# Third layer of a four-layer network: the attention's denominators kept with heads on partitions and spread on strips of the array, and the last batch's squares summed ahead of the down projection

## The reference

```python
def _L2_attn_ref(x, w_qkv, w_out, decay_param):      # 16 heads of 16 channels
    q = _phi(to_bhtd(q))                             # phi(z) = elu(z) + 1
    k = _phi(to_bhtd(k))
    running_kv = _decay_scan(k * v, decay, init)     # s_t = decay * s_{t-1} + x_t
    running_ksum = _decay_scan(k, decay, init)
    den = jnp.clip(jnp.sum(q * running_ksum, axis=-1, keepdims=True), EPS_DEN, None)
    out = q * running_kv / den
    out = out.transpose(0, 2, 1, 3).reshape(B, T, Hid) @ w_out

def _L2_ffn_ref(x, w_gate_up, w_proj):
    h = jax.nn.silu(gate) * up                       # 1024 wide, ternary weights
    hn = rms_norm(h)
    return jnp.einsum('bsd,hd->bsh', hn, wq_p)
```

## Time and profile before

| quantity | us |
|---|---|
| median of 3 runs | 1033.42 |
| lowest and highest of them | 1028.28, 1034.17 |
| the profiled execution's own time | 1029.84 |
| its span, first to last instruction | 1028.0 |
| TensorE busy in the span | 946.4 |
| VectorE busy | 715.1 |
| ScalarE busy | 464.8 |
| GpSimd busy | 435.2 |

### The profile page before, as it was taken

One profiled execution on the slowest core, in us unless ns is written; L12 is line 12 of the kernel. 1 busy time (PEld: TensorE's weight loads), 2 busy tenths in 40 slices (PEclk: granted clock), 3 DMA queues, 4 the chain that ended last, 5 costly groups with the idle time before them and its releaser, 6 DMA issues. The chain is left out here.

```text
span 1028.0 us, 12619 instructions
## 1 busy us (share of the span) xinstructions
PE 946.4 (92%) x4494; PEld 481.0 (47%) x4498; DVE 715.1 (70%) x1327; ACT 464.8 (45%) x767; POOL 435.2 (42%) x444
## 2 busy tenths in 40 slices
PE   4999799879999999878999997999999999999997
PEld 2677555323333333344555646633662474256325
DVE  3777565678888888547777773768586777758674
ACT  2333045247766666645575451621371246134411
POOL 2222357554444333017245361087128505840770
PEclk9999799979999999998999997999999999999999
DMA  8700035312211220030000001000000000000000
GB/s 295 259 16 16 16 105 141 123 40 65 63 47 49 63 63 2 1 146 1 17 16 1 16 1 44 1 0 1 21 1 1 1 21 1 0 1 22 0 1 21
DMA packets 28942, 43.67 MB, mean 42 GB/s; under 512 B 6512, under 2 KB 22080, under 8 KB 28480
## 3 DMA queue, kind: packets, MB, share of 16 engines
q1 hardware_dynamic: 28880, 42.87, 13.4%
HBM read 31.38 MB, written 11.27 MB: 41 GB/s over the span
## 5 line engine op out<-in xcount | busy, mean ns | idle before, releaser
L2180 POOL TENSOR_TENSOR l_scaled<-l_X,l_source 128x512 f32<-128x512 f32 x112 | 135.6, 1240 | 141.6 <-ACT l_X L2250 124.6
L1102 DVE TENSOR_REDUCE l_nmax<-banks 128x1 f32<-128x512 f32 (+1 forms) x165 | 147.7, 929 | 34.9 <-PE banks L1211 33.7
L1057 ACT ACTIVATE l1b_PT<-banks 128x512 f32<-128x512 f32 (+1 forms) x176 | 134.1, 793 | 66.8 <-PE banks L1224 66.4
L1211 PE MATMUL banks<-l_KQ 96*128 96x512 bf16 x240 | 81.3, 392 | 8.6 <-DVE l_nmax L1102 5.8
L1224 PE MATMUL banks<-l_KQ 99*128 99x512 bf16 x256 | 85.0, 385 | 3.0 <-ACT l1b_PT L1057 2.1
L2263 ACT ACTIVATE l_hhi<-l_h 128x512 f16<-128x512 f32 (+1 forms) x24 | 15.1, 630 | 129.4 <-DVE l_h L2375 129.4
L2599 PE MATMUL banks<-l_scaled,l_cbm 128*64 128x512 f32 x224 | 59.5, 613 | 10.7 <-POOL l_scaled L2180 10.6
L1238 PE MATMUL banks<-l1b_PT,l1b_V 128*32 128x512 f32 x512 | 68.2, 605 | 0.0
L2349 DVE TENSOR_TENSOR l_decayed<-banks,l_right_decay 128x512 f32<-128x512 f32 x56 | 38.4, 686 | 37.9 <-PE banks L2599 37.9
L2621 PE MATMUL banks<-l_decayed,w_place 64*128 64x512 f32 x224 | 63.2, 641 | 0.0
L1783 PE MATMUL banks<-l_xhi,l_ternary 128*128 128x512 f16 x128 | 49.8, 389 | 8.6 <-DVE l_h L1713 8.6
(11 more groups left out here) (342 smaller groups left out, 2052.1 us busy)
## 6 DMA issues: line engine op xcount, KB each, us to landing
l_split<-l1a_parts SPq DMA_DIRECT2D x16, 384.0 KB, 3.3
l_KQ<-l_split SPq DMA_DIRECT2D x48, 128.0 KB, 2.9
l_KQ<-l_split SPq DMA_DIRECT2D x16, 192.0 KB, 3.1
l_KQ<-l_split SPq DMA_DIRECT2D x48, 64.0 KB, 2.8
w_ternary<-l_tern_out SPq DMA_DIRECT2D x7, 384.0 KB, 2.3
x<-in_x SPq DMA_DIRECT2D x4, 512.0 KB, 9.4
l_raw<-in_w_gate_up SPq DMA_DIRECT2D x2, 1024.0 KB, 9.9
out<-x SPq DMA_DIRECT2D x4, 512.0 KB, 3.0
```

The costliest lines, as they stand in the source:

```text
L1057: nc.scalar.activation(PT[:, first:first + size, :], source, ACT.Exp, scale=SCALE).then_inc(p_ready, 1)
L1102: nc.vector.tensor_reduce(nmax[:, H % 2, first:first + size], source, axis=AX.X, op=ALU.max, negate=True).then_inc(smax_read, 1)
L1211: last = nc.tensor.matmul(ps[bank + m][:, :], KQ[pairs, QUERY, g, j, t * P:(t + 1) * P], KQ[pairs, KEY, g, j, :], start=True, stop=True)
L2180: nc.gpsimd.tensor_tensor(by_head(scaled[:, (2 * u + m) % 4, :]), by_head(X[:, T, :]), spread(source[:, level, T, :]), ALU.mult).then_inc( ...
```

## The change

The selector gets 32 columns instead of 8 (the further 24 are zeros), and the denominators are made with heads on partitions at once: two products (four instructions) of 512 columns, one on columns 0 to 31 of the array and one on columns 32 to 63, which fill partitions 0 to 63 of bank 6. The column of the ternary mean moves to bank 7. VectorE clips 64 partitions of 512 columns in one instruction and waits for it (semaphore `den_read`). It inverts them in four pieces of 128 columns: one in step j = 4, two in step 5, one in step 6, each behind that step's `h` and `hlo`. `spread_denominators` waits for all four and multiplies 32 rows at a time, on rows 0 to 31 of the array and on rows 32 to 63. `turn_denominators` with its transposes, ScalarE's copy, `rdenT` and two semaphores are gone. In the last batch `sum_squares` comes ahead of `project_gated`, writes to bank 0 instead of 6, and waits for the last `h` instead of for the attention having been added.

```diff
-        rden = sb("rden", [P, TT, L2_HEADS])
-        rdenT = sb("rdenT", [L2_HEADS, S])
+        rden = sb("rden", [CT * GAP, S])
...
-        DEN_AT, RT_AT, SPREAD_AT = 3, 5, 7
+        DEN_AT, SPREAD_AT = 3, 7
+        INVERSE_AT = {DEN_AT + 1: (0,), DEN_AT + 2: (1, 2), DEN_AT + 3: (3,)}
...
+        def squares_bank(b):
+            return 6 if b + 1 < B else 0
...
-                    if j == RT_AT + 1:
-                        act.wait_ge(rt_made, b + 1)
-                        nc.scalar.activation(rdenT[:, :], ps[7][0:L2_HEADS, :], ACT.Copy).then_inc(rt_ready, 1)
...
-                            means.invert(own, ps[6][:, TOTAL:TOTAL + 1])
-                        own.link(nc.vector.tensor_scalar(rden[:, :, :], ps[6][:, 0:TT * L2_HEADS].rearrange("p (t h) -> p t h", t=TT),
-                                                         1e-6, None, ALU.max))
-                        nc.vector.reciprocal(rden[:, :, :], rden[:, :, :]).then_inc(rden_ready, 1)
+                            means.invert(own, ps[7][:, TOTAL:TOTAL + 1])
+                        nc.vector.tensor_scalar(rden[:, :], ps[6][0:CT * GAP, :], 1e-6, None, ALU.max).then_inc(den_read, 1)
+                        dve.wait_ge(den_read, b + 1)
+                    for t in INVERSE_AT.get(j, ()):
+                        nc.vector.reciprocal(rden[:, t * P:(t + 1) * P], rden[:, t * P:(t + 1) * P]).then_inc(rden_ready, 1)
...
-                for t in range(TT):
-                    for c in range(CT):
-                        n = t * L2_HEADS + c * (L2_HEADS // CT)
-                        last = nc.tensor.matmul(ps[6][:, n:n + L2_HEADS // CT], qk[:, c, t * P:(t + 1) * P], w.select[:, :],
-                                                start=True, stop=True)
+                for c in range(CT):
+                    rows = slice(c * GAP, (c + 1) * GAP)
+                    last = nc.tensor.matmul(ps[6][rows, :], w.select[:, :], qk[:, c, :], start=True, stop=True,
+                                            tile_position=(0, c * GAP))
...
-            def turn_denominators(b):
-                pe.wait_ge(rden_ready, b + 1)
-                for t in range(TT):
-                    last = nc.tensor.transpose(ps[7][0:L2_HEADS, t * P:(t + 1) * P], rden[:, t, :], k.ident[:, :])
-                last.then_inc(rt_made, 1)
...
-                pe.wait_ge(rt_ready, b + 1)
+                pe.wait_ge(rden_ready, b * TT + TT)
...
-                    nc.tensor.matmul(ps[4 + c][:, :], w.spread[:, c, :], rdenT[:, :], start=True, stop=True).then_inc(spread, 1)
+                    rows = slice(c * GAP, (c + 1) * GAP)
+                    nc.tensor.matmul(ps[4 + c][:, :], w.spread[rows, :], rden[rows, :], start=True, stop=True).then_inc(spread, 1)
...
-                    pe.wait_ge(aout_added, b * 2 + 2)
+                    pe.wait_ge(h_ready, B * HT)
...
-                project_gated(b)
-                sum_squares(b)
+                    project_gated(b)
+                    sum_squares(b)
+                else:
+                    sum_squares(b)
+                    project_gated(b)
```

More of the change, by code:

```diff
@@ L1340, in _ @@
                 project(B - 1, t, t // 2)
-L2_HEADS, GROUP = 16, 64
+L2_HEADS, GROUP, GAP = 16, 64, 32
 HID = 4 * C
@@ L1355, in weights2 @@
     w.decay = loaded("w2_decay", "w2", [P, CT], aps["w2_decay"])
-    w.select = loaded("w2_select", "w2", [P, P // HEAD], aps["const_select16"])
-    w.spread = loaded("w2_spread", "w2", [L2_HEADS, CT, P], aps["const_spread16"])
+    w.select = loaded("w2_select", "w2", [P, GAP], aps["const_select16"])
+    w.spread = loaded("w2_spread", "w2", [CT * GAP, P], aps["const_spread16"])
     w.group = loaded("w2_group", "small", [P, P], aps["const_group64"])
@@ L1369, in layout2 @@
     a["w2_proj"] = f["L2_ffn_w_proj"].T
-    a["const_select16"] = np.kron(np.eye(P // HEAD), np.ones((HEAD, 1))).astype(np.float32)
-    a["const_spread16"] = np.kron(np.eye(L2_HEADS), np.ones((1, HEAD))).reshape(L2_HEADS, CT, P).astype(np.float32)
+    a["const_select16"] = np.kron(np.eye(P // HEAD, GAP), np.ones((HEAD, 1))).astype(np.float32)
+    a["const_spread16"] = np.tile(np.kron(np.eye(GAP, P // HEAD), np.ones((1, HEAD))), (CT, 1)).astype(np.float32)
     a["const_group64"] = np.kron(np.eye(P // GROUP), np.ones((GROUP, GROUP))).astype(np.float32)
@@ L1516, in layer2 @@
         rden_ready = sem("rden_ready")
-        rt_made = sem("rt_made")
-        rt_ready = sem("rt_ready")
+        den_read = sem("den_read")
         spread = sem("spread")
@@ L1690, in norm_gated @@
                 dve.wait_ge(ss_made, b + 1)
-                nc.vector.tensor_scalar(inv[:, :], ps[6][:, 0:TT], 1.0 / HID, float(np.finfo(np.float32).eps),
+                nc.vector.tensor_scalar(inv[:, :], ps[squares_bank(b)][:, 0:TT], 1.0 / HID, float(np.finfo(np.float32).eps),
                                         ALU.mult, ALU.add).then_inc(ss_ready, 1)
@@ L1799, in denominators @@
                     pe.wait_ge(means.summed, b + 1)
-                    nc.tensor.matmul(ps[6][:, TOTAL:TOTAL + 1], k.ones[:, :], means.total[:, :], start=True,
+                    nc.tensor.matmul(ps[7][:, TOTAL:TOTAL + 1], k.ones[:, :], means.total[:, :], start=True,
                                      stop=True).then_inc(total_made, 1)
-            def turn_denominators(b):
-                pe.wait_ge(rden_ready, b + 1)
-                for t in range(TT):
-                    last = nc.tensor.transpose(ps[7][0:L2_HEADS, t * P:(t + 1) * P], rden[:, t, :], k.ident[:, :])
-                last.then_inc(rt_made, 1)
             def spread_denominators(b):
-                pe.wait_ge(rt_ready, b + 1)
+                pe.wait_ge(rden_ready, b * TT + TT)
                 if b:
@@ L1842, in sum_squares @@
                 else:
-                    pe.wait_ge(aout_added, b * 2 + 2)
+                    pe.wait_ge(h_ready, B * HT)
                 for t in range(TT):
-                    last = nc.tensor.matmul(ps[6][:, t:t + 1], sqsum[:, t * P:(t + 1) * P], k.ones[:, 0:1], start=True, stop=True)
+                    last = nc.tensor.matmul(ps[squares_bank(b)][:, t:t + 1], sqsum[:, t * P:(t + 1) * P], k.ones[:, 0:1], start=True, stop=True)
                 last.then_inc(ss_made, 1)
@@ L1857, in _ @@
                         denominators(b)
-                    if j == RT_AT:
-                        turn_denominators(b)
                     if j == SPREAD_AT:
```

## The result

The changed kernel takes 1036.85 us (median of 18 runs, 1033.61 to 1043.04); the kernel before, over 18 runs, 1030.13 (1027.88 to 1034.54). The runs of the kernel before lie near 1029 or near 1034 with little between, so its median jumps from set to set (1029.35, 1033.74 and 1033.72 in the three later ones) while its mean stays within 1030.9 to 1032.1; the ratios go with the means. The ratio is 1.0064, with a 95% interval of 1.0045 to 1.0083: 6.6 us slower, with 4.6 to 8.5 as bounds. The forecast was 1044.5, and its sum +11.1 us; the range of 1036 to 1052 holds the time by 0.85 us. Against the 1030.13 of these runs 1044.5 is +14.4 us, where +6.7 was measured. The direction was right and the size was wrong.

A forecast was written before the change was run, and what follows sets the result against it. TensorE was taken to bound the kernel (busy 946.4 of 1028.0 us), waiting for VectorE in the gate steps. Later projections 5.5, low clock 5.3 and last batch 0.3 gave +11.1 us, forecast 1044.5 us (range 1036 to 1052).

The forecast's parts named there:

- the base on which the sum was set: Whole kernel: profiled execution of 1029.84 us, raised by 3.6 us because the median of the runs lay above it.
- the path on VectorE: Third layer, gate step 4 to projection: VectorE's added work starts each projection 1.84 us later, 5.5 us for three batches.
- The reciprocals: VectorE, gate steps 4 to 6: each piece of 128 columns costs 0.95 us, by 6.25 ns a column.
- The estimate of 8.3 ns a column: VectorE's reciprocal as iterated divide, repeat count 8: 4 us more over four batches than the forecast, which followed the rows.
- the meeting of `hlo` with GpSimd's additions: Second batch, step 5: the next `hlo` waits for two GpSimd additions ending at 521.43, VectorE free at 521.90.
- The clock: TensorE's projection behind the waits: one clock fall a batch, 1.77 us each, 5.3 us in three batches.
- Rival 2: Third layer's batches: two stretches of low clock each, lasting into the projection; +16.4 us, 1050; chance 0.10.
- The last batch and the tail: Third layer's end: projection about 2.4 us later, moved squares give back 2.1 us, leaving +0.3.
- The strips: TensorE's denominators and spread on two strips: denominators in 1.0 us, gain 0.7; spread gains 0.9 a batch.
- The sum: Whole kernel: 5.5 + 5.3 + 0.3 = +11.1 us, 1040.9; with 3.6 for the median 1044.5, 1.1% slower.

The follow-up runs named there:

- filled: The changed kernel with ten further matmuls, read by nobody, between gate step 7 and the spread of each batch; 0.9999 of the kernel before (0.9975 to 1.0024).
- the denominators alone: The changed kernel with the last batch's squares put back behind the down projection; 1041.36 us, 1.0101 of the kernel before (1.0056 to 1.0146).

## Where the prediction was wrong, and what it had right

The mechanism was right: late pieces of the reciprocal, a wait ahead of the spread, a low clock behind it. Two steps of the working failed, and both made the forecast too high: the base on which the sum was set (3.3 us of the 7.7 by which it was too high), and the path on VectorE, which was given 1.84 us a batch where 1.2 were measured (1.9 us).

- **The reciprocals: right.** 0.95 us a piece was predicted by the line through three rows; 0.925 on average was measured, and 0.95 against 0.94 for 128 and 64 partitions. The estimate of 8.3 ns a column, worked out from the Trainium skill (VectorE: DVE Perf Modes, the section on the fixed hardware budget), would have made about 1.2 of it (128 x 2.1 ns more than 0.95); the trace disagrees with it.
- **The path on VectorE: right in kind, a third too long.** Each batch's projection was to start 1.84 us later; where the clock holds it starts 1.2 later (16.13 and 16.14 against 14.93). The step that failed here is the meeting of `hlo` with GpSimd's additions. I took the two additions of 3.04 us from the trace of before and had step 5's `hlo` wait for their end. But the first of the two had been slowed itself: it took 1.62 us beside the `hlo` of step 4, which had begun 0.18 ahead of it. In the changed kernel that `hlo` came sooner, the additions took 1.34 and 1.27, and they were all but over when step 5's `hlo` came (0.70). Step by step against my path, 0.2 of the 0.6 is this meeting, 0.2 the silu of step 4, which was done sooner, and the rest small differences up to the projection. For three batches 3.6 us instead of 5.5.
- **The clock: right in kind.** One fall a batch at 1.77 us, 5.3 in all, was the term. The ratios of filled and the changed kernel put it at 6.7, with all four batches in it. In the traces of the changed kernel a fall costs between 0.8 and 2.4 us: the second batch stands 45.33 us from the third and the third 46.96 from the fourth, where filled has 44.55 at full clock for both. The difference is how long the clock stays low. In the second batch it is back behind 530.5 us, in the third it is low for twice as long:

```profile
530.50:533.00 2.50, 2.50 (x14) 2.19 (x13) 0.79 (x2) 0.00 (x0) 2.42 (x2) 1.00 0.00 0
571.50:578.00 6.50, 6.50 (x19) 4.46 (x20) 4.00 (x6) 1.75 (x3) 3.79 (x4) 0.50 0.00 0
```

The first and the fourth batch are like the third, and both traces of the changed kernel agree in this. So Rival 2 (the low clock lasts twice as long) holds for three batches of four in these traces, though the whole time stays below its 1050; and one fall a batch, my term, is no rule either, as the first two batches of the denominators alone had the waits and no fall behind them. What decides between these cases I can't say from the runs. The sentence drawn from the Trainium skill (TensorE: Matmul & The Clock Gate, Part 4), that transposes don't count as busy in the same way, is neither shown nor refuted.
- **The last batch and the tail: right.** The squares ahead of the projection gave 2.0 us (2.1 predicted), and the projection started 1.9 us later in filled (16.14 against 14.23 from gate step 3), 2.4 predicted.
- **The strips: right, and worth nothing by themselves.** 1.05 us shown for four instructions of the denominators, 1.13 for the spread at full clock. What TensorE was spared went into its waits.
- **The sum: too high by its base more than by any of its terms.** 1044.5 was 7.7 us too high. I had added 3.6 us because the median of three runs lay above the profiled execution; over these 18 runs that median is 1030.13, 0.3 above the profiled 1029.84, so the base carries 3.3 of the 7.7. The path on VectorE carries 1.9 (5.5 against 3.6), the last batch 0.4 (+0.3 against 1.9 - 2.0), the clock 0.4 (5.3 against 6.7 less the 1.8 that the last batch lost in the kernel before already). With the terms as measured the sum is 8.4, where the ratio gives 6.6 and its interval ends at 8.5; the runs don't account for the last 1.8. The base was bad luck in part: the three runs had caught two of the high ones, and in two of the three later sets the median of the kernel before was 1033.7. What failed is to set a sum read from one execution on a median that the choice of runs moves by 4 us.

## What to carry to other kernels

A cheap operation on one engine is not cheap when the shape it works on changes: the reciprocal is paid by its columns, so turning 128 x 64 into 64 x 512 made 3.7 us of 0.55; look for the layout that fills all partitions before moving an operation to save a transpose. When an engine that is waited for gets more work, count the clock too: here the 1.2 us a batch by which the projection was late (4.8 in four) cost rather less than the low clock behind it (6.7 by the ratios, with 3 to 10 as bounds), and ten useless matmuls in the gap took back the whole loss. And a base for a difference needs more than three runs where single runs spread by 6 us; even the medians of some twenty runs differed by 4 us here. Compare means of many runs, taken in the same session.

## What the runs showed of the hardware

- The layers ahead of the change, the same instructions in every kernel, end between 439.1 and 447.8 us in twelve traces; low stretches of TensorE's granted clock need not fall in the same places (at 119 to 125 us the clock was 0.50 in one trace of the changed kernel and 1.00 in the other). A difference of a few us between two traces says nothing until the stretches without a low clock are compared.
- The length of a wait doesn't foretell the clock. 1.65 us directly ahead of the projection, behind the thin spread and the transposes, were followed by a projection of 6.36 us, and so were 1.28 us ahead of the spread with 0.51 ahead of the projection (6.35). 2.48 us ahead of the spread gave 4.28 us in one batch and 5.09 in the next, and in the denominators alone 3.72 at full clock.
- An operation on VectorE with two operands in SBUF is held by GpSimd's additions (0.68 us alone, 1.06 to 1.77 in their company), while the reciprocal, with one operand, took 0.94 us beside an addition of 1.27. The addition is not always as quick there: one that ran beside two reciprocals and a product that reads a bank (522.95 in the changed kernel) took 1.71, and why no run shows.
